# Attention scores from one matmul of full 32-bit operands, in place of three of high and low parts

## The chip, the cores and the metric

The kernel runs on one core of one Trainium2 chip. The metric is the device time of one execution in microseconds (us). The core has five engines that run side by side and meet only at semaphores: TensorE (PE in the rows; its weight loads are PEld), VectorE (DVE), ScalarE (ACT), GpSimd (POOL) and SyncE (SP), which here only issues DMAs.

## The reference

`x` is 64 sequences of 512 rows by 512 features; the context is 64 x 77 rows by 512. What is computed, cut to the parts that matter:

```
h      = layernorm(x)
q      = h @ Wq          16 query heads of 32, in 4 groups for each of 4 key heads
k, v   = ctx @ Wk, ctx @ Wv      4 heads of 32
scores = rope(q) . rope(k)       queries summed over their group; 77 context rows for each head
o      = mean over heads of softmax(scores / sqrt(32)) @ v
x1     = x + o @ Wo
x2     = x1 + ffn(layernorm(x1))     8-bit inputs, weights of -1, 0, 1, one global scale
```

## The kernel before, in words

The work has three stages, one after the other, as the program on each engine is written by hand.

**The context stage** runs over 39 tiles of 128 context rows (the last has 64). For each tile TensorE transposes the context (L1054), multiplies it by the weights of keys and values (L1065, 12 matmuls, also of high and low parts, which the change does not touch), and transposes the rotated keys (L1073). ScalarE copies the transposed keys out of PSUM as float32r, a form that is rounded to fewer mantissa bits and takes one matmul record (`keys_out`, L595): this is the high part. VectorE subtracts it from the full value in PSUM and keeps the rest as the low part (`low_keys`, L787). SyncE stores both to the scratch tensor `k_scr` (L331 in the loop, L365 at its end), after it has stored the values (L330), and loads the context four tiles ahead (L324). SyncE does all of this in the order of the program.

**The attention stage** runs over 128 steps, each a pair of 128-row tiles of `x`. It is a software pipeline: in step i, projection works on pair i, scores on i-1, values on i-2, the head sum on i-3, the residual on i-4, and statistics on i-5. TensorE's order within a step is: transposes of `x` (L1138), of rotated queries (L1150) and of the attention output (L1158), the query projection (L1168, full 32-bit), the output projection (L1179), transposes of the exponentials (L1189), the scores (L1203), the value products (L1216, full 32-bit). The scores of a pair are two PSUM banks, one for each tile, 308 columns wide: 4 heads x 77 context rows, with the keys laid out block-diagonally in `k_blk`. Each bank takes three matmuls: high query x low key, low x high, high x high. The high query part is ScalarE's copy (L653), the low part VectorE's subtraction (L912), which also signals `qlo_ready`. SyncE loads the keys of each sequence into `k_blk` in four pieces (L400), one for each head, and the values in six (L404).

**The last stage** quantises, transposes, and multiplies by the ternary weights (f16, L1248). It reads nothing that the change touches.

`low_keys` is called once for each context tile, and L912 once for each step of the attention stage.

Of the kernel before, what the change touches and what calls it, by code (L numbers as in the profile page):

```python
# [32 lines left out]
CTX = 77  # L33
HEADS, GROUPS, D = 4, 4, 32
HD = HEADS * D

P = 128
# [6 lines left out]
SC = HEADS * CTX  # L44
# [46 lines left out]
def build(nc, x, ctx_in, wq, wk, wv, wo, fw, fb, ident_d, qcos_d, qsin_d, kcos_d, ksin_d, out):  # L91
# [11 lines left out]
    with stack:  # L103
        def sb(name, shape, dt=F32):
            return stack.enter_context(nc.sbuf_tensor(name, shape, dt))
# [4 lines left out]
        def sem(name):  # L110
            return stack.enter_context(nc.semaphore(name))


        k_scr = nc.dram_tensor("k_scr", (P, 2, CROWS), F32, kind="Internal").ap()
        v_scr = nc.dram_tensor("v_scr", (CROWS, HEADS, VC), F32, kind="Internal").ap()


# [8 lines left out]
        q_sb = sb("q_sb", [P, 2 * HD])  # L126
        qa_sb = sb("qa_sb", [P, 2 * HD])
        qb_sb = sb("qb_sb", [P, 2 * HD])
        qT_sb = sb("qT_sb", [P, 2, 2 * P], F32R)
        e_sb = sb("e_sb", [P, 2, 2, SC])  # L130
        pT_sb = sb("pT_sb", [P, 2, CHUNKS * P])
        pv_sb = sb("pv_sb", [P, 2, HEADS, VC])
# [3 lines left out]
        ost_sb = sb("ost_sb", [P, 2, 2, 2, D], F32R)  # L136
        oT_sb = sb("oT_sb", [P, 2, P], F32R)
        sq_sb = sb("sq_sb", [P, E], BF16)
        k_blk = sb("k_blk", [P, 2, 2, SC])
        v_blk = sb("v_blk", [P, 2, CHUNKS, HEADS, VC])  # L140
        bn_sb = sb("bn_sb", [P, 2, 6])
        mv_sb = sb("mv_sb", [P, 2, 2])
# [48 lines left out]
        ka_sb = early(2, HD)  # L191
        kb_sb = early(2, HD)
        kr_sb = early(2, HD)
        kT_sb = early(2, 2, P)
        kT_r = kT_sb.bitcast(F32R)
        v_sb = early(4, HEADS, VC)
        vw_sb = early(2, HEADS, D)
        wo4 = early(E)
# [38 lines left out]
        cT_done, cT_copied, kv_done, kr_ready, v_ready, v_copied, kT_done, kT_copied, kv_read = (  # L237
            sem(n) for n in ("cT_done", "cT_copied", "kv_done", "kr_ready", "v_ready", "v_copied",
                             "kT_done", "kT_copied", "kv_read"))
        k_copied, k_mul, klo_ready, qlo_ready = (sem(n) for n in ("k_copied", "k_mul", "klo_ready", "qlo_ready"))  # L240
        whi_ready, wlo_ready, clo_ready = sem("whi_ready"), sem("wlo_ready"), sem("clo_ready")

        stats_ready, rs_ready = sem("stats_ready"), sem("rs_ready")
# [64 lines left out]
        def _(sp):  # L308
# [15 lines left out]
                sp.dma_start(ctx_sb[0:rows, n, :], ctx_rows[bass.ds((j + 4) * P, rows), :]).then_inc(c_in[n], 16)  # L324

            def kv_store(j, n):
                sp.wait_ge(klo_ready, j - 1)
                sp.wait_ge(v_copied, j + 1)
                sp.wait_ge(v_ready, j + 1)
                sp.dma_start(v_scr[bass.ds(j * P, P), :, :], v_sb[:, n, :, :]).then_inc(v_out[n], 16)  # L330
                sp.dma_start(k_scr[:, :, bass.ds((j - 2) * P, P)], kT_sb[:, n % 2, :, :])\  # L331
                  .then_inc(k_out[n % 2], 16)

            sp.wait_ge(zeroed, ZEROED)
# [22 lines left out]
            for j in range(groups * 4, CT + 3):  # L357
                if j + 4 <= CT:
                    ctx_load(j, j % 4, P if j + 4 < CT else CLAST)
                if j in (CT - 5, CT - 2):  # L360
                    b = 1 + (j == CT - 2)
                    sp.dma_start(x_sb[:, b, :, :], xv[b]).then_inc(x_in[b], 16)
                rows = P if j - 2 < CT else CLAST
                sp.wait_ge(klo_ready, j - 1)
                sp.dma_start(k_scr[:, :, (j - 2) * P:(j - 2) * P + rows], kT_sb[:, j % 2, :, 0:rows])\  # L365
                  .then_inc(k_out[j % 2], 16)
                if j <= CT:
                    rows = P if j < CT else CLAST
                    sp.wait_ge(v_copied, j + 1)
                    sp.wait_ge(v_ready, j + 1)  # L370
                    sp.dma_start(v_scr[j * P:j * P + rows, :, :], v_sb[0:rows, j % 4, :, :])\
                      .then_inc(v_out[j % 4], 16)
# [23 lines left out]
            def kv_step(b, k):  # L396

                at_least(sp, sc_done_t, 4 * (b - 2) + 4)
                for h in range(HEADS):
                    sp.dma_start(k_blk[D * h:D * h + D, k % 2, :, CTX * h:CTX * h + CTX],  # L400
                                 k_scr[D * h:D * h + D, :, bass.ds(b * CTX, CTX)]).then_inc(k_in[k % 2], 16)
                at_least(sp, pv_done, 2 * (b - 2) + 2)
                for c, r, n, h, a in SEGS:
                    sp.dma_start(v_blk[r:r + n, k % 2, c, h, :], v_scr[bass.ds(b * CTX + a, n), h, :])\  # L404
                      .then_inc(v_in[k % 2], 16)
# [52 lines left out]
        def _(pool):  # L458
            pool.memset(ones_sb[:, :], 1.0).then_inc(zeroed, 1)
            pool.memset(v_sb[:, :, :, D + 1:D + 2], 1.0).then_inc(zeroed, 1)  # L460
            pool.memset(k_blk[:, :, :, :], 0.0).then_inc(zeroed, 1)
            pool.memset(v_blk[:, :, :, :, :], 0.0).then_inc(zeroed, 1)
            pool.memset(mhalf[:, :], -0.5).then_inc(zeroed, 1)
            pool.memset(bones[:, :], 0.0).then_inc(zeroed, 1)
# [97 lines left out]
        def _(act):  # L562
# [26 lines left out]
            def keys_out(j, m, g, rows=P):  # L589

                act.wait_ge(kT_done, j + 1)

                at_least(act, k_out[m], 16 * g)

                act.activation(kT_r[:, m, 0, 0:rows], bank[4 + m][:, 0:rows], ACT.Copy).then_inc(kT_copied, 1)  # L595

            ctx_step(0, 0)
            for j in range(4):
# [24 lines left out]
            def step(i, k, g):  # L623
# [21 lines left out]
                if score:  # L645
                    j, kj, gj = score
                    act.wait_ge(qT_done, j + 1)
                    if resid:

                        act.wait_ge(oT_done, resid[0] + 1)  # L650

                    at_least(act, sc_done_t, 2 * j)
                    act.activation(qT_sb[:, 0, :], bank[3][:, 0:2 * P], ACT.Copy).then_inc(qT_copied, 1)  # L653
                if resid:
                    j, kj, gj = resid
                    act.wait_ge(oT_done, j + 1)
# [79 lines left out]
        def _(dve):  # L736
# [44 lines left out]
                dve.tensor_reduce(v_sb[0:rows, n, :, D:D + 1].rearrange("p h a -> p (h a)"),  # L781
                                  vw_sb[0:rows, n % 2, :, :], AX.X, ALU.add).then_inc(v_ready, 1)

            def low_keys(j, n, rows=P):

                dve.wait_ge(kT_copied, j + 1)
                dve.tensor_tensor(kT_r[:, n, 1, 0:rows], bank[4 + n][:, 0:rows], kT_sb[:, n, 0, 0:rows],  # L787
                                  ALU.subtract).then_inc(klo_ready, 1)

            wq_groups = [wq_sb[:, :, :, g, :].rearrange("p c h d -> p (c h) d") for g in range(GROUPS)]  # L790
            wq_sum = wqs[:, :, :].rearrange("p c (h d) -> p (c h) d", h=HEADS)
            for j in range(CHEAD):
                if j >= 1:
                    low_ctx(j + 1, (j + 1) % 2)
                ctx_step(j, j % 4, j // 4)
                if j >= 2:
                    low_keys(j - 2, j % 2)

                if j == 5:
                    dve.wait_ge(wq_in, 16)  # L800
                    then(dve.tensor_tensor(wq_sum, wq_groups[0], wq_groups[1], ALU.add))
# [31 lines left out]
            with dve.Fori(CHEAD // 4, CTAIL // 4) as g:  # L833
                for n in range(4):
                    low_ctx(g * 4 + n + 1, (n + 1) % 2)
                    ctx_step(g * 4 + n, n, g)
                    low_keys(g * 4 + n - 2, n % 2)
            for j in range(CTAIL, CT + 3):
                if j < CT:
                    low_ctx(j + 1, (j + 1) % 2, P if j + 1 < CT else CLAST)  # L840
                if j <= CT:
                    ctx_step(j, j % 4, j // 4, P if j < CT else CLAST)
                if j - 2 < CT:
                    low_keys(j - 2, j % 2)
                o = j - CTAIL
                if o == 0:

# [18 lines left out]
            def step(i, k, g):  # L866
# [20 lines left out]
                if proj:  # L887
                    j, kj, gj = proj
                    dve.bn_stats(bn_sb[:, 1, :], x_sb[:, kj // 2, 2 * (kj % 2) + 1, :]).then_inc(bn_step, 1)  # L889
                    if isinstance(j, int) and j == 0:  # L890

                        low_keys(CT, CT % 2, CLAST)
                    dve.wait_ge(bn_step, 2 * j + 2)
                if stat:

# [9 lines left out]
                if score:  # L905

                    j, kj, gj = score
                    if resid:
                        dve.wait_ge(oT_copied, resid[0] + 1)
                    else:  # L910
                        dve.wait_ge(qT_copied, j + 1)
                    dve.tensor_tensor(qT_sb[:, 1, :], bank[3][:, 0:2 * P], qT_sb[:, 0, :].bitcast(F32),  # L912
                                      ALU.subtract).then_inc(qlo_ready, 1)
                if proj:
                    j, kj, gj = proj

# [128 lines left out]
        def _(pe):  # L1045
# [23 lines left out]
            def ctx_kT(j, n, rows=P):  # L1069
                m = n % 2  # L1070
                pe.wait_ge(kr_ready, j + 1)
                at_least(pe, klo_ready, j - 1)
                pe.transpose(bank[4 + m][:, 0:rows], kr_sb[0:rows, m, :], ident[0:rows, 0:rows])\  # L1073
                  .then_inc(kT_done, 1)

# [49 lines left out]
            def step(i, k, g):  # L1125
# [66 lines left out]
                if score:  # L1192
                    j, kj, gj = score
                    slot = kj // 2 % 2
                    if kj % 2 == 0:

                        pe.wait_ge(k_in[slot], gj * (2 * K_DMAS * 16) + (kj // 4 + 1) * (K_DMAS * 16))

                    at_least(pe, sub_done_t, 2 * j)
                    pe.wait_ge(qlo_ready, j + 1)  # L1200
                    for t in range(2):
                        for n, (a, b) in enumerate(((0, 1), (1, 0), (0, 0))):
                            last = pe.matmul(bank[4 + t][:, 0:SC], qT_sb[:, a, t * P:(t + 1) * P],  # L1203
                                             k_blk[:, slot, b, :].bitcast(F32R), start=n == 0, stop=n == 2)
                        last.then_inc(sc_done_t, 1)
                if value:
                    j, kj, gj = value
                    slot = kj // 2 % 2
# [100 lines left out]
```

## Time and profile before

| | |
|---|---|
| median of 3 runs | 1320.23 us (1318.98 to 1321.29) |
| the profiled execution's own time | 1319.5 us |
| its span, first to last instruction | 1317.7 us |
| mean granted TensorE clock | 0.99 of full speed |
| PE busy | 1267.9 us (96%), x9848 |
| PEld busy | 1085.9 us (82%), x9911 |
| DVE busy | 1181.8 us (90%), x2772 |
| ACT busy | 1025.1 us (78%) |
| POOL busy | 791.2 us (60%) |

The spans of records on one engine overlap in the trace, since matmuls and vector operations are pipelined. So the distance from start to start tells what a record costs its engine, and the record's own duration does not. A full 32-bit matmul of the program stands as two records in the trace: the query projection is 128 x 2 x 4 = 1024 matmuls of the program and x2048 records.

### The profile page before, as it was taken

Reading aid. Unit: us, or ns where it says so; the run is one execution under the profiler, and the core shown is the slowest. Engines: PE = TensorE matmul, PEld = TensorE weight load, DVE = VectorE, ACT = ScalarE, POOL = GpSimd, SP = SyncE. Lnnn points to the kernel's source line nnn. Section 1 sums busy time; section 2 is a strip of 40 time slices with the busy share of each in tenths; the row PEclk is TensorE's granted clock in tenths of the full one; section 3 lists DMA queues with packets and bytes.
Section 4 is the critical chain, followed back from the end, with each engine's and each line's share of the span. In section 5 each row is a group of like instructions: output and inputs, shape, how many; then the busy total and the mean of one; then the engine's idle time right before and its main releaser. Section 6 shows DMA issues by size and latency. Waiting matters only on the chain.

```text
span 1317.7 us, 36811 instructions
## 1 busy us (share of the span) xinstructions
PE 1267.9 (96%) x9848; PEld 1085.9 (82%) x9911; DVE 1181.8 (90%) x2772; ACT 1025.1 (78%) x2338; POOL 791.2 (60%) x1536
## 2 busy tenths in 40 slices
PE   5897999999999999999999999999969999999998
PEld 5796999999999999999999999999935555555554
DVE  4876899999999999999999999999978888888887
ACT  3454788888888888888888888888857878888886
POOL 3564888888888888888888888888820000000000
PEclk9999999999999999999999999999979999999999
DMA  8574355555555555555546452323108999999945
GB/s 266 166 216 133 107 158 182 154 183 161 176 165 171 165 171 167 170 171 166 178 159 187 150 169 76 102 80 98 37 5 332 400 401 395 401 399 404 406 201 223
DMA packets 100815, 265.18 MB, mean 201 GB/s; under 512 B 49705, under 2 KB 65769, under 8 KB 72114
## 3 DMA queue, kind: packets, MB, share of 16 engines
q1 hardware_dynamic: 100786, 264.86, 58.8%
q8 instruction: 10, 0.16, 0.1%
q14 instruction: 19, 0.16, 0.0%
HBM read 139.64 MB, written 125.17 MB: 201 GB/s over the span
## 4 chain that ended last, share of the span: by engine, by line
DVE 47%; PE 31%; issue 15%; DMA 2%; DVEq 2%; SPq 1%; ACT 1%; POOL 1%; POOLq 0%; ACTq 0%
PE bank L1248 18%; DVE amax L898 10%; DVE x_sb L930 8%; DVE e_sb L944 6%; DVE mx_sb L940 5%; DVE bn_sb L889 5%; PE bank L1239 4%; PE bank L1246 3%; DVE qT_sb L912 2%; PE bank L1065 2%; DVE rinv_sb L886 2%; DVE ve_sb L918 2%; DVE bn_sb L881 2%; DVE mv_sb L904 1%; DMA x_sb<-in_ctx 1%
## 5 line engine op out<-in xcount | busy, mean ns | idle before, releaser
L1248 PE MATMUL bank<-wT,x_sb 128*128 128x512 f16 x1024 | 263.9, 380 | 3.5 <-issue 0.2
L1168 PE MATMUL bank<-wqs,xT_sb 128*128 128x128 f32 x2048 | 259.7, 280 | 0.2
L718 ACT ACTIVATE x_sb<-bank,mean,cols 128x512 f32<-128x512 f32 x256 | 196.0, 774 | 67.6 <-PE bank L1248 67.3
L1168 PEld LDWEIGHTS bank<-wqs,xT_sb 128*128 128x128 f32 x2048 | 238.2, 191 | 7.1 <-ACT xT_sb L640 0.8
L1216 PE MATMUL bank<-v_blk,pT_sb 103*128 103x136 f32 x1536 | 199.0, 279 | 0.3 <-ACT pT_sb L682 0.3
L1216 PEld LDWEIGHTS bank<-v_blk,pT_sb 103*128 103x128 f32 x1536 | 190.6, 190 | 0.5 <-ACT pT_sb L682 0.5
L1248 PEld LDWEIGHTS bank<-wT,x_sb 128*128 128x128 f16 x1024 | 100.5, 98 | 106.8 <-issue 1.6
L930 DVE SCALAR_TENSOR_TENSOR x_sb<-x_sb,negm,bank 128x512 f32 (+1 forms) x256 | 179.5, 742 | 7.9 <-PE bank L1179 2.7
L898 DVE TENSOR_REDUCE amax<-x_sb (+1 forms) x128 | 156.0, 1218 | 23.2 <-DVE bn_sb L889 8.0
L691 ACT ACTIVATE sq_sb<-x_sb 128x512 bf16 (+1 forms) x256 | 161.4, 631 | 18.7 <-DVE x_sb L930 1.4
L1005 DVE TENSOR_TENSOR x_sb<-x_sb 128x512 f32 (+1 forms) x256 | 164.5, 683 | 1.2 <-ACT x_sb L718 1.2
L682 ACT ACTIVATE pT_sb<-bank 103x384 f32<-103x384 f32 x256 | 111.7, 489 | 53.1 <-PE bank L1189 53.1
L640 ACT ACTIVATE xT_sb<-bank 128x512 f32<-128x512 f32 x256 | 138.9, 595 | 7.6 <-PE bank L1138 3.0
L1203 PE MATMUL bank<-k_blk,qT_sb 128*128 128x308 f32 x768 | 140.1, 317 | 1.8 <-DMA k_blk<-k_scr 1.8
L504 POOL TENSOR_TENSOR rs<-ve_sb,mhalf 128x2 f32 (+1 forms) x128 | 89.5, 700 | 79.9 <-DVE ve_sb L875 79.9
L1138 PE MATMUL bank<-ident,x_sb 128*128 128x128 f32 x1024 | 133.0, 273 | 0.0
L667 ACT ACTIVATE e_sb<-e_sb,rs_sb 128x308 f32<-128x308 f32 x256 | 129.2, 568 | 0.0
L997 DVE TENSOR_SCALAR x_sb<-bank 128x1024 f16<-128x1024 f16 x128 | 88.5, 691 | 44.6 <-PE bank L1239 43.0
L940 DVE TENSOR_REDUCE mx_sb<-bank 128x4 f32<-128x308 f32 x256 | 110.1, 471 | 11.0 <-PE bank L1203 8.1
L1138 PEld LDWEIGHTS bank<-ident,x_sb 128*128 128x128 f32 x1024 | 117.0, 141 | 0.0
L1203 PEld LDWEIGHTS bank<-k_blk,qT_sb 128*128 128x128 f32 x768 | 111.0, 189 | 2.2 <-DMA k_blk<-k_scr 2.0
L1189 PEld LDWEIGHTS bank<-ident,e_sb 128*103 128x103 f32 x768 | 98.5, 168 | 15.4 <-issue 1.3
(126 smaller groups left out, 2584.4 us busy)
## 6 DMA issues: line engine op xcount, KB each, us to landing
out_y<-x_sb SPq DMA_DIRECT2D x112, 1024.0 KB, 7.2
x_sb<-in_x SPq DMA_DIRECT2D x64, 1024.0 KB, 6.5
x_sb<-out_y SPq DMA_DIRECT2D x48, 1024.0 KB, 9.0
x_sb<-in_ctx SPq DMA_DIRECT2D x38, 256.0 KB, 2.8
k_blk<-k_scr SPq DMA_DIRECT2D x256, 19.2 KB, 5.5
k_scr<-x_sb SPq DMA_DIRECT2D x38, 128.0 KB, 2.3
v_scr<-x_sb SPq DMA_DIRECT2D x38, 68.0 KB, 2.3
v_blk<-v_scr SPq DMA_DIRECT2D x128, 10.2 KB
```

Source lines behind the costliest of these rows:

```text
L640: act.activation(xT_sb[:, t, :, :].rearrange("p c r -> p (c r)"), bank[t][:, :], ACT.Copy).then_inc(xT_copied_t, 1)
L691: act.activation(sq_sb[:, :], x1_at(kj, gj, t), ACT.Square, accum_out=ssq[:, bass.ds(2 * j + t, 1)]).then_inc(sq_done, 1)
L718: act.activation(u_sb[:, t, :], bank[4 + t][:, :], ACT.Identity, bias=stat_of(mean1, j, t, back), scale=cols[:, 6:7]).then_inc(scaled_t, 1)
L898: dve.tensor_reduce(amax[:, bass.ds(2 * j, 2)], x1_at(kj, gj).rearrange("p (t e) -> p t e", t=2), AX.X, ALU.max, apply_absolute_value=True ...
L930: dve.scalar_tensor_tensor(out=x1_at(kj, gj, t), in0=x_sb[:, kj // 2, 2 * (kj % 2) + t, :], scalar=negm[:, kj, t:t + 1], in1=bank[t][:, :] ...
L940: dve.tensor_reduce(mx_sb[:, t, :], bank[4 + t][:, 0:SC].rearrange("p (h a) -> p h a", h=HEADS), AX.X, ALU.max).then_inc(mx_ready, 1)
L1005: dve.tensor_tensor(x1_tile, x1_tile, u_sb[:, t, :], ALU.add).then_inc(sum_done_t, 1)
L1138: last = pe.transpose(bank[t][:, c * P:(c + 1) * P], x_sb[:, kj // 2, 2 * (kj % 2) + t, c * P:(c + 1) * P], ident[:, :])
L1168: last = pe.matmul(bank[2][:, t * HD:(t + 1) * HD], xT_sb[:, t, c, :], wqs[:, c, :], start=c == 0, stop=c == EC - 1)
L1203: last = pe.matmul(bank[4 + t][:, 0:SC], qT_sb[:, a, t * P:(t + 1) * P], k_blk[:, slot, b, :].bitcast(F32R), start=n == 0, stop=n == 2)
L1216: last = pe.matmul(bank[6][:, t * HEADS * VC:(t + 1) * HEADS * VC], pT_sb[0:CR, t, c * P:(c + 1) * P], v_blk[0:CR, slot, c, :, :].rearrang ...
L1248: last = pe.matmul(bank[4 + t][:, :], q16T_sb[:, t, c, :], wT[:, c, :], start=False, stop=c == EC - 1)
```

## The change

The keys and queries are no longer split. `kT_sb`, `k_scr`, `k_blk` and `qT_sb` lose the dimension that held the two parts, and hold plain float32. `low_keys` and the subtraction of L912 are gone from VectorE, with their semaphores `klo_ready` and `qlo_ready`; whoever waited for these now waits for ScalarE's copies, `kT_copied` and `qT_copied`. The scores of each tile are one matmul of float32 operands.

```diff
-        k_scr = nc.dram_tensor("k_scr", (P, 2, CROWS), F32, kind="Internal").ap()
+        k_scr = nc.dram_tensor("k_scr", (P, CROWS), F32, kind="Internal").ap()
...
-        qT_sb = sb("qT_sb", [P, 2, 2 * P], F32R)
+        qT_sb = sb("qT_sb", [P, 2 * P])
...
-        k_blk = sb("k_blk", [P, 2, 2, SC])
+        k_blk = sb("k_blk", [P, 2, SC])
...
             def kv_store(j, n):
-                sp.wait_ge(klo_ready, j - 1)
+                sp.wait_ge(kT_copied, j - 1)
...
-                sp.dma_start(k_scr[:, :, bass.ds((j - 2) * P, P)], kT_sb[:, n % 2, :, :])\
+                sp.dma_start(k_scr[:, bass.ds((j - 2) * P, P)], kT_sb[:, n % 2, :])\
...
-                    sp.dma_start(k_blk[D * h:D * h + D, k % 2, :, CTX * h:CTX * h + CTX],
-                                 k_scr[D * h:D * h + D, :, bass.ds(b * CTX, CTX)]).then_inc(k_in[k % 2], 16)
+                    sp.dma_start(k_blk[D * h:D * h + D, k % 2, CTX * h:CTX * h + CTX],
+                                 k_scr[D * h:D * h + D, bass.ds(b * CTX, CTX)]).then_inc(k_in[k % 2], 16)
...
-                act.activation(kT_r[:, m, 0, 0:rows], bank[4 + m][:, 0:rows], ACT.Copy).then_inc(kT_copied, 1)
+                act.activation(kT_sb[:, m, 0:rows], bank[4 + m][:, 0:rows], ACT.Copy).then_inc(kT_copied, 1)
...
-                    act.activation(qT_sb[:, 0, :], bank[3][:, 0:2 * P], ACT.Copy).then_inc(qT_copied, 1)
+                    act.activation(qT_sb[:, :], bank[3][:, 0:2 * P], ACT.Copy).then_inc(qT_copied, 1)
...
-            def low_keys(j, n, rows=P):
-
-                dve.wait_ge(kT_copied, j + 1)
-                dve.tensor_tensor(kT_r[:, n, 1, 0:rows], bank[4 + n][:, 0:rows], kT_sb[:, n, 0, 0:rows],
-                                  ALU.subtract).then_inc(klo_ready, 1)
...
-                    if resid:
-                        dve.wait_ge(oT_copied, resid[0] + 1)
-                    else:
-                        dve.wait_ge(qT_copied, j + 1)
-                    dve.tensor_tensor(qT_sb[:, 1, :], bank[3][:, 0:2 * P], qT_sb[:, 0, :].bitcast(F32),
-                                      ALU.subtract).then_inc(qlo_ready, 1)
...
-                at_least(pe, klo_ready, j - 1)
+                at_least(pe, kT_copied, j - 1)
...
-                    pe.wait_ge(qlo_ready, j + 1)
-                    for t in range(2):
-                        for n, (a, b) in enumerate(((0, 1), (1, 0), (0, 0))):
-                            last = pe.matmul(bank[4 + t][:, 0:SC], qT_sb[:, a, t * P:(t + 1) * P],
-                                             k_blk[:, slot, b, :].bitcast(F32R), start=n == 0, stop=n == 2)
-                        last.then_inc(sc_done_t, 1)
+                    pe.wait_ge(qT_copied, j + 1)
+                    for t in range(2):
+                        pe.matmul(bank[4 + t][:, 0:SC], qT_sb[:, t * P:(t + 1) * P], k_blk[:, slot, :],
+                                  start=True, stop=True).then_inc(sc_done_t, 1)
```

TensorE, in a full step of the attention stage, from the output projection to the first value product; before:

```order
L1179 MATMUL bank<-wst,oT_sb 128x512 [waits oT_copied]
L1179 MATMUL bank<-wst,oT_sb 128x512
L1189 MATMUL bank<-ident,e_sb 103x128 [waits exp_done_t,pv_copied]
L1189 MATMUL bank<-ident,e_sb 103x128 x5
L1203 MATMUL bank<-k_blk,qT_sb 128x308 [waits qlo_ready,sub_done_t]
L1203 MATMUL bank<-k_blk,qT_sb 128x308 x5
L1216 MATMUL bank<-v_blk,pT_sb 128x136 [waits pT_copied_t,v_in1]
```

The same place in the changed kernel, whose line numbers are smaller:

```order
L1154 MATMUL bank<-wst,oT_sb 128x512 [waits oT_copied]
L1154 MATMUL bank<-wst,oT_sb 128x512
L1164 MATMUL bank<-ident,e_sb 103x128 [waits exp_done_t,pv_copied]
L1164 MATMUL bank<-ident,e_sb 103x128 x5
L1177 MATMUL bank<-k_blk,qT_sb 128x308 [waits qT_copied,sub_done_t]
L1177 MATMUL bank<-k_blk,qT_sb 128x308
L1189 MATMUL bank<-v_blk,pT_sb 128x136 [waits pT_copied_t,v_in1]
```

Six matmuls of the program have become two at the same place, and nothing else in the step has moved.

VectorE, in the same steady step, from the maximum of absolute values (L898) to the row maximum of the scores (L940); before:

```order
L898 TENSOR_REDUCE amax<-x_sb 128x2 [waits added_t,bn_step]
L904 BN_AGGR mv_sb<-bn_sb 128x2 x2
L912 TENSOR_TENSOR qT_sb<-bank,qT_sb 128x256 [waits oT_copied]
L918 TENSOR_SCALAR ve_sb<-mv_sb 128x2 [waits mv_ready]
L920 TENSOR_SCALAR negm<-mv_sb 128x2
L930 SCALAR_TENSOR_TENSOR x_sb<-x_sb,negm,bank 128x512 [waits y_done_t]
```

In the changed kernel, at that place:

```order
L882 TENSOR_REDUCE amax<-x_sb 128x2
L888 BN_AGGR mv_sb<-bn_sb 128x2 x2
L893 TENSOR_SCALAR ve_sb<-mv_sb 128x2 [waits mv_ready]
L895 TENSOR_SCALAR negm<-mv_sb 128x2
```

The subtraction and its wait are gone, and the two small operations behind it have moved up.

SyncE, in the loop of the context stage: a context load, the store of the values, and the store of the keys; before:

```order
L324 DMA x_sb<-in_ctx 128x512
L330 ISA [waits v_ready,v_copied,klo_ready]
L330 DMA v_scr<-x_sb 128x136
L331 ISA
L331 DMA k_scr<-x_sb 256x1x128
```

In the changed kernel:

```order
L323 DMA x_sb<-in_ctx 128x512
L329 ISA [waits v_ready,v_copied,kT_copied]
L329 DMA v_scr<-x_sb 128x136
L330 ISA
L330 DMA k_scr<-x_sb 128x128
```

The store of the keys has half as many rows, and the wait ahead of the store of the values asks for ScalarE's copy in place of VectorE's subtraction.

## Rows read from the trace of the kernel before

**Rows 1.** Windows: us, busy us (records) of each engine, granted clock, DMA share, GB/s
```profile
0.00:126.00 126.00, 98.81 (x750) 91.46 (x751) 83.92 (x209) 55.49 (x169) 63.08 (x136) 0.97 0.68 203
126.00:955.00 829.00, 827.80 (x6817) 805.86 (x6815) 791.55 (x2014) 690.24 (x1757) 720.14 (x1384) 1.00 0.48 147
...
977.00:1317.00 340.00, 331.26 (x2233) 181.98 (x2294) 290.46 (x510) 267.81 (x382) 0.00 (x0) 0.99 0.86 346
```

**Rows 2.** Waits from 300 to 900 us: total us, times, longest us
```profile
ACT pv_sb L631 <- PE bank L1216: 22.0, 92, 0.3
ACT q_sb L674 <- PE bank L1168: 20.5, 91, 0.2
```

**Rows 3.** The chain from 147.5 to 156 us: start us, us, what
```profile
147.80 0.47 PE bank L1179 x2
148.27 0.65 PE bank L1189 x6
148.92 0.86 PE bank L1203 x6
149.78 1.39 PE bank L1216 x12
151.17 0.88 PE bank L1138 x8
152.05 0.22 PE bank L1150 x2
...
152.49 1.86 PE bank L1168 x16
```

**Rows 4.** The page's chain by engine, over the whole span
```profile
DVE 47%; PE 31%; issue 15%; DMA 2%; DVEq 2%; SPq 1%; ACT 1%; POOL 1%; POOLq 0%; ACTq 0%
```

**Rows 5.** VectorE's timeline in one step: start us, us, line, operation
```profile
600.11 0.39 DVE L912 TENSOR_TENSOR qT_sb<-bank,qT_sb 128x256 fp32r<-128x256 f32 x1
600.42 0.30 DVE L918 TENSOR_SCALAR ve_sb<-mv_sb 128x2 f32<-128x2 f32 x1
...
600.84 1.41 DVE L930 SCALAR_TENSOR_TENSOR x_sb<-x_sb,negm,bank 128x512 f32 x2
602.24 0.86 DVE L940 TENSOR_REDUCE mx_sb<-bank 128x4 f32<-128x308 f32 x2
...
606.64 0.39 DVE L912 TENSOR_TENSOR qT_sb<-bank,qT_sb 128x256 fp32r<-128x256 f32 x1
```

**Rows 6.** TensorE's timeline in the same step
```profile
601.03 1.10 PE L1203 MATMUL bank<-k_blk,qT_sb 128*128 128x308 f32 x6
```

**Rows 7.** Groups by line and shape: records | busy us, mean ns | idle before
```profile
L1248 PE MATMUL bank<-wT,x_sb 128*128 128x512 f16 x1024 | 263.9, 380 | 3.5 <-issue 0.2
...
L1216 PE MATMUL bank<-v_blk,pT_sb 103*128 103x136 f32 x1536 | 199.0, 279 | 0.3 <-ACT pT_sb L682 0.3
L1203 PE MATMUL bank<-k_blk,qT_sb 128*128 128x308 f32 x768 | 140.1, 317 | 1.8 <-DMA k_blk<-k_scr 1.8
...
L1239 PE MATMUL bank<-ident,x_sb 128*128 128x128 f16 x1024 | 78.9, 220 | 2.5 <-ACT x_sb L708 2.3 <-DVE x_sb L1015 0.2
```

**Rows 8.** The chain from 0 to 126 us, shares by line
```profile
by line: PE bank L1065 18.6%; DMA x_sb<-in_ctx 12.7%; DVE cT_parts L753 6.4%; PE bank L1054 6.4%; issue 5.4%; DVE x_sb L776 4.7%; DMA x_sb<-in_wv 3.9%; DVE x_sb L787 3.3%; DMA k_scr<-x_sb 3.3%; DVE x_sb L781 3.1%; SPq L331 2.7%; DVE x_sb L8
```

**Rows 9.** SyncE's timeline in the context stage
```profile
86.41 0.35 SPq L330 DMA_DIRECT2D v_scr<-x_sb  x1
86.94 0.59 SPq L331 DMA_DIRECT2D k_scr<-x_sb  x1
```

**Rows 10.** SyncE's timeline at the start of the attention stage
```profile
120.45 2.61 SPq L400 DMA_DIRECT2D k_blk<-k_scr  x4
123.10 2.29 SPq L404 DMA_DIRECT2D v_blk<-v_scr  x6
```

More of the change, by code:

```diff
@@ L193, in build @@
         kr_sb = early(2, HD)
-        kT_sb = early(2, 2, P)
-        kT_r = kT_sb.bitcast(F32R)
+        kT_sb = early(2, P)
         v_sb = early(4, HEADS, VC)
@@ L239, in build @@
                              "kT_done", "kT_copied", "kv_read"))
-        k_copied, k_mul, klo_ready, qlo_ready = (sem(n) for n in ("k_copied", "k_mul", "klo_ready", "qlo_ready"))
+        k_copied, k_mul = sem("k_copied"), sem("k_mul")
         whi_ready, wlo_ready, clo_ready = sem("whi_ready"), sem("wlo_ready"), sem("clo_ready")
@@ L363, in _ @@
                 rows = P if j - 2 < CT else CLAST
-                sp.wait_ge(klo_ready, j - 1)
-                sp.dma_start(k_scr[:, :, (j - 2) * P:(j - 2) * P + rows], kT_sb[:, j % 2, :, 0:rows])\
+                sp.wait_ge(kT_copied, j - 1)
+                sp.dma_start(k_scr[:, (j - 2) * P:(j - 2) * P + rows], kT_sb[:, j % 2, 0:rows])\
                   .then_inc(k_out[j % 2], 16)
@@ L460, in _ @@
             pool.memset(v_sb[:, :, :, D + 1:D + 2], 1.0).then_inc(zeroed, 1)
-            pool.memset(k_blk[:, :, :, :], 0.0).then_inc(zeroed, 1)
+            pool.memset(k_blk[:, :, :], 0.0).then_inc(zeroed, 1)
             pool.memset(v_blk[:, :, :, :, :], 0.0).then_inc(zeroed, 1)
@@ L795, in _ @@
                 ctx_step(j, j % 4, j // 4)
-                if j >= 2:
-                    low_keys(j - 2, j % 2)
                 if j == 5:
@@ L836, in _ @@
                     ctx_step(g * 4 + n, n, g)
-                    low_keys(g * 4 + n - 2, n % 2)
             for j in range(CTAIL, CT + 3):
@@ L842, in _ @@
                     ctx_step(j, j % 4, j // 4, P if j < CT else CLAST)
-                if j - 2 < CT:
-                    low_keys(j - 2, j % 2)
                 o = j - CTAIL
@@ L889, in step @@
                     dve.bn_stats(bn_sb[:, 1, :], x_sb[:, kj // 2, 2 * (kj % 2) + 1, :]).then_inc(bn_step, 1)
-                    if isinstance(j, int) and j == 0:
-                        low_keys(CT, CT % 2, CLAST)
                     dve.wait_ge(bn_step, 2 * j + 2)
@@ L904, in step @@
                         dve.bn_aggr(mv_sb[:, t, :], bn_sb[:, t, :]).then_inc(mv_ready, 1)
-                if score:
-                    j, kj, gj = score
-                    if resid:
-                        dve.wait_ge(oT_copied, resid[0] + 1)
-                    else:
-                        dve.wait_ge(qT_copied, j + 1)
-                    dve.tensor_tensor(qT_sb[:, 1, :], bank[3][:, 0:2 * P], qT_sb[:, 0, :].bitcast(F32),
-                                      ALU.subtract).then_inc(qlo_ready, 1)
                 if proj:
```

## The prediction

> **What bounds the kernel now.** I read the windows first, to know which stage the change falls in. The attention stage fills 829 of the 1317.7 us, and in it TensorE is busy for 827.80 at a granted clock of 1.00, which is the level of 2.4 GHz [rows 1]. The last stage, 340 us, touches nothing that is changed. Next the waits: over 600 us of the attention stage ScalarE waits for TensorE at two places in nearly every step, 0.2 us at each [rows 2], and no row has TensorE waiting for anyone. Then the chain, where it runs through TensorE: the pieces of a step follow each other without a gap, and L1203 is one of them with 0.86 us [rows 3] (0.85 in other steps). The pieces add up to one step: 0.47 + 0.65 + 0.86 + 1.39 + 0.88 + 0.22 + 0.22 (L1158, the same as L1150) + 1.86 = 6.55 us.
>
> Against this stands the chain over the whole span, which gives VectorE 47% and TensorE 31% [rows 4]. VectorE is busy for 791.55 of the 829 us [rows 1], so the two engines run neck and neck. Which one holds the other is to be seen in one step: the scores' records end at 601.03 + 1.10 = 602.13, and VectorE's row maximum, which needs them, starts at 602.24 [rows 5, 6]. The operation before it, L930, ends at 600.84 + 1.41 = 602.25. VectorE is thus released by TensorE at about the moment at which it would be free anyway, and its next wait is so short that it shows as no gap. I take TensorE as the engine that sets the step: its pieces stand at the pace of their columns and it waits for nobody.
>
> **The scores, the term that decides.** Now they are six records of 308 columns: 0.855 us for six, 0.1425 each [rows 3]. After, each program matmul of full 32-bit operands is two records, so there are four in a step. No row has such a record of 308 columns. The nearest is the value product, L1216, with 136 columns: 1.39 / 12 = 0.116 us from start to start [rows 3]. Is that pace set by the columns, and how often do they pass? The durations tell: f16 records take 220 ns with 128 columns and 380 with 512, so 0.417 ns for each column [rows 7]. A single pass of 136 columns would be 220 + 8 x 0.417 = 223 ns; the row has 279, which is 220 + 144 x 0.417 = 280, that is 272 columns. So a record of full 32-bit operands passes its columns twice. The pace agrees: 272 x 0.417 = 113 ns and some 2.5 ns more is the 116 seen. For 308 columns this gives 616 x 0.417 + 2.5 = 259 ns; scaled in proportion from L1216 it would be 0.116 x 308 / 136 = 0.262. I take 0.260: four records take 1.04 us in place of 0.855, so 0.185 us more a step, and 128 x 0.185 = **+23.7 us**.
>
> Two pages of the Trainium skill speak to this and don't agree. "FP8 and Floating Point Precision", section "TensorE Precision Notes", has true FP32 pass the array four times, which would make the sum what it is. "Perfetto Trace Analysis", section "Engine Utilization", only halves the output rate for FP32_LOW_HIGH; read as two passes for the whole matmul, it would make this change a gain (rival 1).
>
> **Bounds of that term.** Below: 616 x 0.417 with nothing on top, 257 ns, gives 4 x 0.257 - 0.86 = 0.168 a step, +21.5 us. Above: the one-pass records that the kernel has now are slower than their columns, 0.1425 where 308 x 0.417 + 2.5 is 0.131, so by 9%. L1216 shows no such loss, but it is short. With 9% on 259 the record is 0.282, and the step 0.273 longer: +35 us.
>
> **The wait before the scores.** TensorE waited for `qlo_ready`, now for `qT_copied`, which comes sooner. The subtraction ends at 600.11 + 0.39 = 600.50 and the scores start at 601.03 [rows 5, 6], so nothing hung on it. No gain.
>
> **VectorE.** It loses L912, which holds it for 0.31 us a step (L912 starts at 600.11, the next operation at 600.42) [rows 5]. Its own work fits in a step already, and TensorE's step grows to 6.55 + 0.185 = 6.73. So this becomes idle time: L930 may start earlier only if the output projection is done, and the row maximum must wait for the scores, which come 0.185 later. Late next after the maximum are the reciprocal for GpSimd and the statistics; both move with TensorE's step. Gain 0. If VectorE were the true bound, see rival 3.
>
> **The context stage.** Here TensorE is busy for 98.81 of 126 us [rows 1], and other work on the chain shrinks. The subtraction L787 holds 3.3% of 126 us, 4.2 us, and it goes wholly. The issue of the store of keys, L331, holds 2.7%, 3.4 us [rows 8]. It takes 0.59 us where the value store, which has 128 rows as the new one will, takes 0.35 [rows 9]: 0.24 / 0.59 of 3.4 is 1.4 us. At the start of the attention stage four loads of keys take 2.61 us to issue, 0.65 each, and those of values 2.29 / 6 = 0.38 [rows 10]; three of them stand on the chain ahead of the first scores: 3 x 0.27 = 0.8 us. Together 6.4 us if all of it is kept. Not all will be: where L787 goes, L1065 or a context load is late next. Nothing kept would be the other bound. I keep 4.5 us, about two thirds, since TensorE has slack of about a fifth there: **-4.5 us**. Loads and stores of keys move half the bytes; in the attention stage DMA is busy for 0.48 of the time [rows 1] and nobody on TensorE waits for it, so that is 0.
>
> **The sum.** 1319.5 us (the profiled execution) + 23.7 - 4.5 = 1338.7. The median of the runs is 0.7 us above the profiled one, so 1339.4; I say 1339.5 us, +1.5%.
>
> **Rivals.**
> 1. *Full 32-bit records pass their columns once, and their pace so far is set by the weight load.* For it: all records of 128 and 136 columns stand at 0.110 to 0.116 us (0.88 / 8, 1.39 / 12), as if by a common floor [rows 3]. Against it: the durations of 279 against 220 ns [rows 7]. Then a record of 308 columns costs what it does now, 0.1425, and four 0.57: -0.285 a step, -36.5 us, and 1320.2 - 36.5 - 4.5 = 1279 us. It decides from a pace below 0.855 / 4 = 0.214 us for the stage alone, and 0.214 + 4.5 / 512 = 0.223 with the context stage's gain. This is what the halved rate of "Perfetto Trace Analysis" would bring; the durations of this trace speak against it. Chance 5%.
> 2. *The long record loses 9% as the one-pass records do.* 1320.2 + 35 - 3 = 1352 us. Against it: L1216 at its columns' pace. Chance 9%.
> 3. *VectorE holds the step today.* For it: its 47% of the chain [rows 4] and 791.55 of 829 us. Then its 0.31 us fall out, and TensorE's own floor decides. In a step that is 6.55 less the one slack that its pieces show: L1168's 1.86 against 16 records of 256 x 0.417 + 2.5 = 109 ns, so 0.115. Then 6.435 + 0.185 = 6.62, +0.07 a step, +9 us: 1320.2 + 9 - 4.5 = 1325 us. Chance 8%.
> 4. *No difference:* a pace near 0.22 us, for which no row speaks. 2%.
>
> **Chances and range.** My forecast has 76%, with a range of its own of 1334 to 1343 us (term of the scores 21.5 to 26, the context stage 2 to 6.4). Reaching part of the way to rivals 3 and 2, since between them and the forecast mixtures can lie, the range is 1329 to 1347 us; what it leaves out is rival 1, most of 2 and 3, and 4, under 2 in 10 with what the mixtures hold back. A measurement of this kernel can tell about 0.2%, 2.6 us, from no change. Faster by more than that: 5% (rival 1). Within it: 3% (rival 4, and a little for a sum of small errors). Slower: 92%.
>
> **What would show each step.** In the changed kernel's trace: the scores as x512 records in all, 259 to 262 ns from start to start, with a mean duration near 430 (220 + 488 x 0.417 = 423 and a little for the first of a step); in the chain, four records with 1.04 us; a step of 6.73 us; TensorE without waits, and VectorE with a new wait of 0.1 to 0.3 us a step at the row maximum or at L930, for TensorE; the stage of the context shorter by 2 to 6 us, with the store of keys issued in about 0.36 us. I am wrong if the four records take 0.6 us (rival 1) or 1.13 (rival 2), or if the step is shorter than 6.55 + 0.15 although the records are as foretold (rival 3).

## The result, and the profile after

| | before | changed |
|---|---|---|
| median | 1319.61 us (1318.84 to 1321.29, 4 runs) | 1336.53 us (1334.67 to 1339.28, 4 runs) |
| profiled execution | 1319.5 us | 1337.84 us |
| span | 1317.7 us | 1336.0 us |
| VectorE busy | 1181.8 us | 1161.8 us |

The ratio is 1.0127, with a 95% interval of 1.0114 to 1.014: 15 to 18.5 us slower. The forecast was 1339.5 us, in a range of 1329 to 1347.

The chain of the changed kernel, one step of the attention stage (start us, us, what):

```profile
606.67 0.88 PE bank L1113 x8
607.55 0.22 PE bank L1125 x2
607.76 0.22 PE bank L1133 x2
607.98 1.87 PE bank L1143 x16
609.85 0.47 PE bank L1154 x2
610.31 0.66 PE bank L1164 x6
610.97 1.04 PE bank L1177 x4
612.01 1.39 PE bank L1189 x12
613.40 0.11 PE bank L1113
```

Against [rows 3] one piece has changed: the scores are four records with 1.04 us, where six had 0.86. From one group of transposes of `x` to the next it is 613.40 - 606.67 = 6.73 us, against 6.55.

The page of the changed kernel, its chain over the whole span, and the groups of the scores and of VectorE's row maximum:

```profile
PE 92%; DVE 3%; DMA 1%; issue 1%; ACT 1%; POOL 1%; SPq 1%; POOLq 0%; DVEq 0%; ACTq 0%
...
L1177 PE MATMUL bank<-k_blk,qT_sb 128*128 128x308 f32 x512 | 153.9, 423 | 0.0
...
L915 DVE TENSOR_REDUCE mx_sb<-bank 128x4 f32<-128x308 f32 x256 | 110.6, 474 | 36.9 <-PE bank L1177 34.4
```

The same place of the kernel before, from its view of L940 (what VectorE sat idle for ahead of the row maximum: us, times):

```profile
  PE bank L1203: 8.1, 6
```

The chain has moved from VectorE (47% in [rows 4]) to TensorE. VectorE now waits for the scores, 34.4 us in all. In the kernel before it had 8.1 us of this wait, at 6 places; in the other steps the wait was too short to be told from the end of L930. One step of VectorE in the changed kernel shows the new wait:

```profile
603.73 1.40 DVE L905 SCALAR_TENSOR_TENSOR x_sb<-x_sb,negm,bank 128x512 f32 x2
605.39 0.86 DVE L915 TENSOR_REDUCE mx_sb<-bank 128x4 f32<-128x308 f32 x2 [0.25 <-PE bank L1177]
```

To part the stages, take the first and the last group of transposes of `x` in the attention stage. TensorE's timeline before:

```profile
113.76 1.04 PE L1138 MATMUL bank<-ident,x_sb 128*128 128x128 f32 x8
...
943.98 1.04 PE L1138 MATMUL bank<-ident,x_sb 128*128 128x128 f32 x8
```

and in the changed kernel:

```profile
110.79 1.04 PE L1113 MATMUL bank<-ident,x_sb 128*128 128x128 f32 x8
...
963.07 1.04 PE L1113 MATMUL bank<-ident,x_sb 128*128 128x128 f32 x8
```

The attention stage starts 3.0 us earlier. Its 127 steps take 852.28 us in place of 830.22: 22.1 us more, 0.174 a step. What lies behind the last group is 372.9 us in place of 373.7. So -3.0 + 22.1 - 0.8 = +18.3 us, the difference of the spans.

The first steps fill the pipeline and differ from the rest. In the middle, from 300 to 900 us, the mean step is 6.551 us before and 6.728 in the changed kernel: 0.177 more. The scores and the transposes ahead of them can be parted from the other pieces. In one step, TensorE's timeline before and then changed:

```profile
148.11 0.82 PE L1189 MATMUL bank<-ident,e_sb 128*103 128x128 f32 x6
...
149.62 1.55 PE L1216 MATMUL bank<-v_blk,pT_sb 103*128 103x136 f32 x12
```

```profile
145.99 0.82 PE L1164 MATMUL bank<-ident,e_sb 128*103 128x128 f32 x6
...
147.68 1.55 PE L1189 MATMUL bank<-v_blk,pT_sb 103*128 103x136 f32 x12
```

From the first of these starts to the second is 1.51 and 1.69 us. Over the 90 steps in the middle the means are 1.508 and 1.693 us, so the scores cost 0.185 us more. The output projection ahead of them, from its start to that of the transposes, takes 0.555 and 0.547 us, which gives 0.008 back.

SyncE in the changed kernel, in the context stage and at the start of the attention stage:

```profile
80.27 0.34 SPq L329 DMA_DIRECT2D v_scr<-x_sb  x1
80.80 0.34 SPq L330 DMA_DIRECT2D k_scr<-x_sb  x1
...
115.00 1.74 SPq L399 DMA_DIRECT2D k_blk<-k_scr  x4
```

The store of keys is issued in 0.34 us in place of 0.59 [rows 9], four loads of keys in 1.74 in place of 2.61 [rows 10].

### The profile page after: what moved, and what is told of

It is laid out like the page before. It is cut to its first block, busy times and chain, and to the rows that moved or that the text cites. A ratio compares the mean times of both kernels' runs of the same rounds, so it can differ in the third digit from the quotient of the medians.

```text
span 1336.0 us, 36113 instructions
## 1 busy us (share of the span) xinstructions
PE 1289.9 (97%) x9592; PEld 1075.9 (81%) x9655; DVE 1161.8 (87%) x2605; ACT 1025.0 (77%) x2338; POOL 790.1 (59%) x1536
## 4 chain that ended last, share of the span: by engine, by line
PE 92%; DVE 3%; DMA 1%; issue 1%; ACT 1%; POOL 1%; SPq 1%; POOLq 0%; DVEq 0%; ACTq 0%
PE bank L1143 18%; PE bank L1221 17%; PE bank L1189 13%; PE bank L1177 10%; PE bank L1113 8%; PE bank L1164 6%; PE bank L1154 4%; PE bank L1212 4%; PE bank L1219 3%; PE bank L1040 2%; PE bank L1125 2%; PE bank L1133 2%; DMA x_sb<-in_ctx 1%; PE bank L1029 1%; DVE cT_parts L752 1%
## 5 line engine op out<-in xcount | busy, mean ns | idle before, releaser
L1189 PEld LDWEIGHTS bank<-v_blk,pT_sb 103*128 103x128 f32 x1536 | 197.1, 190 | 18.0 <-ACT pT_sb L681 0.5
L1189 PE MATMUL bank<-v_blk,pT_sb 103*128 103x136 f32 x1536 | 199.2, 279 | 0.3 <-ACT pT_sb L681 0.3
L1177 PE MATMUL bank<-k_blk,qT_sb 128*128 128x308 f32 x512 | 153.9, 423 | 0.0
L915 DVE TENSOR_REDUCE mx_sb<-bank 128x4 f32<-128x308 f32 x256 | 110.6, 474 | 36.9 <-PE bank L1177 34.4
L919 DVE TENSOR_TENSOR e_sb<-bank,mx_sb 128x308 f32<-128x308 f32 x256 | 109.4, 470 | 0.0
```

Source lines behind the costliest of these rows:

```text
L1177: pe.matmul(bank[4 + t][:, 0:SC], qT_sb[:, t * P:(t + 1) * P], k_blk[:, slot, :], start=True, stop=True).then_inc(sc_done_t, 1)
L1189: last = pe.matmul(bank[6][:, t * HEADS * VC:(t + 1) * HEADS * VC], pT_sb[0:CR, t, c * P:(c + 1) * P], v_blk[0:CR, slot, c, :, :].rearrang ...
```

## The experiments

Theory T: TensorE sets the step, and the time follows from the pace of its score records; what VectorE is freed from stays hidden. The first rival, V, is that VectorE held the step before. Each ratio is against the kernel before, timed beside the experiment (medians 1320.2 to 1320.4 us).

### VectorE's subtraction put back

```diff
+                if score:
+                    j, kj, gj = score
...
+                    dve.tensor_tensor(qlo_sb[:, :], bank[3][:, 0:2 * P], qT_sb[:, :],
+                                      ALU.subtract).then_inc(qlo_ready, 1)
...
-                    pe.wait_ge(qT_copied, j + 1)
+                    pe.wait_ge(qlo_ready, j + 1)
```

> The changed kernel with VectorE's subtraction of the queries put back: it reads the same bank, writes a tile that nobody reads, and TensorE waits for it ahead of the scores as before. The scores stay one full 32-bit matmul for each tile. Theory T (TensorE sets the step, VectorE's 0.31 us a step were and are hidden): the step stays at 6.73 us and the time at that of the changed kernel, 1336.5 us within 2. Rival V (VectorE sets or shares the step, so that freeing it gave something back): the step grows by 0.1 to 0.3 us, the time by 13 to 38 us to 1350 or more.

1335.66 us, ratio 1.0122 (1.0107 to 1.0138); the changed kernel has 1.0127. The operation costs nothing where it stood. Rival V falls on this side.

### The subtraction taken from the kernel before

```diff
-                    dve.tensor_tensor(qT_sb[:, 1, :], bank[3][:, 0:2 * P], qT_sb[:, 0, :].bitcast(F32),
-                                      ALU.subtract).then_inc(qlo_ready, 1)
...
-                    pe.wait_ge(qlo_ready, j + 1)
+                    pe.wait_ge(qT_copied, j + 1)
...
-                        for n, (a, b) in enumerate(((0, 1), (1, 0), (0, 0))):
+                        for n, (a, b) in enumerate(((0, 1), (0, 0), (0, 0))):
```

> The kernel before with the subtraction of the queries taken out and nothing else moved: still six one-pass records in a step, of which the second of each tile takes the high query part and the high keys in place of the low part and the high keys, so the low part of the queries is left out and the main product counts twice. Theory T: VectorE only hugged TensorE, so the step stays at 6.55 us and the time at 1319.6 within 2; the chain over the span moves from VectorE to TensorE. Rival V: VectorE held the step, its 0.31 us fall out and TensorE's floor of 6.44 decides, so 1305 us.

1318.68 us, ratio 0.9993 (0.9982 to 1.0004): no difference. Its page, the chain over the span:

```profile
PE 87%; DVE 6%; DMA 2%; issue 2%; SPq 1%; ACT 1%; POOL 1%; DVEq 0%; POOLq 0%; ACTq 0%
```

With the time unchanged, the chain went from 47% VectorE to 87% TensorE. So the 47% of [rows 4] said that VectorE had no visible gap, not that it held the step.

### The attention stage changed alone

```diff
-                        for n, (a, b) in enumerate(((0, 1), (1, 0), (0, 0))):
-                            last = pe.matmul(bank[4 + t][:, 0:SC], qT_sb[:, a, t * P:(t + 1) * P],
-                                             k_blk[:, slot, b, :].bitcast(F32R), start=n == 0, stop=n == 2)
-                        last.then_inc(sc_done_t, 1)
+                        pe.matmul(bank[4 + t][:, 0:SC], qT_sb[:, t * P:(t + 1) * P], k_blk[:, slot, 0, :],
+                                  start=True, stop=True).then_inc(sc_done_t, 1)
```

> The kernel before with the attention stage alone changed: full 32-bit queries, one full 32-bit matmul for each tile, no subtraction of the queries. The context stage stays as before: keys split, both parts stored and loaded; the low part of the keys is loaded and not used. Theory T: the attention stage as in the changed kernel, step 6.73 us, and the context stage as in the kernel before, its first transposes of x 3.0 us later than in the changed kernel (113.8 us against 110.8 in the two traces), so 1339.5 us. Rival C (those 3 us are chance of one profile and the two stages differ by nothing): the same as the changed kernel, 1336.5. Rival D (halved key loads helped the attention stage): a step longer than 6.73.

1341.39 us, ratio 1.0177 (1.0161 to 1.0193), 5.7 us over the first experiment, which was timed beside it and differs from it by the keys and by the hidden subtraction. That is more than the 3.0 us expected. Its attention stage starts at 113.31 us, that one's at 110.22. Over all profiles with unsplit keys (nine) the start lies at 110.2 in the mean, over those with split keys (five) at 113.8: the context stage is 3.6 us shorter. The start varies from profile to profile, from 107.3 to 111.5 us with unsplit keys and from 113.3 to 114.5 with split ones, but the two groups don't overlap. The steady step is 6.733 us against 6.726, under a microsecond in all, so rival D has at most that there. The first four steps take 24.8 us against 23.2, which is 1.6 us more. This is not shown to come from the loads of keys: the changed kernel, whose loads are halved as well, takes 24.8 us for them too. The medians lie 1 us further apart than the two profiled spans, which is within the spread of the runs.

### Each score matmul in two halves, and in four quarters

```diff
-                        pe.matmul(bank[4 + t][:, 0:SC], qT_sb[:, t * P:(t + 1) * P], k_blk[:, slot, :],
-                                  start=True, stop=True).then_inc(sc_done_t, 1)
+                        for c in range(2):
+                            last = pe.matmul(bank[4 + t][:, c * (SC // 2):(c + 1) * (SC // 2)],
+                                             qT_sb[:, t * P:(t + 1) * P],
+                                             k_blk[:, slot, c * (SC // 2):(c + 1) * (SC // 2)],
+                                             start=True, stop=True)
+                        last.then_inc(sc_done_t, 1)
```

and with 4 in place of 2.

> The changed kernel with each full 32-bit score matmul cut into two of 154 columns: eight records in a step in place of four, with the same columns in all and twice the weight loads. Theory T (pace is 2 x columns x 0.417 ns and about 2.5 ns): a record is 131 ns, eight are 1.05 us against 1.04, the step grows by 0.01 us, the time by 1 to 2 us. Rival L (a record costs by its weight load or a fixed price, with columns counted once): eight records cost up to twice four, so up to 1 us more a step and 100 us more.

> The changed kernel with each full 32-bit score matmul cut into four of 77 columns: sixteen records in a step. By columns alone a record would be 2 x 77 x 0.417 + 2.5 = 67 ns and sixteen 1.07 us. But all records with 128 weight columns of 32 bits in the trace stand at 109 ns or more, also transposes whose columns would allow it if they passed once. Theory T with a floor for the weight load of 0.109: sixteen take 1.74 us, the step grows by 0.70 us to 7.43, the time by 90 us to 1427. Rival F (no floor, columns alone): the step grows by 0.03, the time by 4 us.

Halves: 1337.53 us (ratio 1.0137, 1.0122 to 1.0153), 131 ns a record. Quarters: 1430.7 us (1.0839, 1.0823 to 1.0856). The pieces of the scores in the chain and their records (duration in ns: min/median/max), of the halves and then of the quarters:

```profile
604.95 1.05 PE bank L1178 x8
...
L1178 PE MATMUL bank<-k_blk,qT_sb x1024: 292/294/398, 121.5 to 975.4; 128*128 128x154 f32 x171
```

```profile
609.20 1.74 PE bank L1178 x16
...
L1178 PE MATMUL bank<-k_blk,qT_sb x2048: 232/275/398, 117.5 to 1065.7; 128*128 128x77 f32 x187
```

1.05 / 8 = 0.131 us for 154 columns is 308 x 0.417 + 2.5 ns: the columns count twice, and the number of records and weight loads nothing. 1.74 / 16 = 0.109 for 77 columns is not 154 x 0.417 + 2.5 = 67 ns but a floor. So both regimes exist, and records of 308 columns are far from the floor.

That the floor is the weight load is not shown. "TensorE: Matmul & The Clock Gate" of the Trainium skill, section "LDWEIGHTS (loading the stationary operand)", prices a load by its columns, which is 107 ns for 128; the pace of 109 lies near that. But the load's own record in this run lasts 192 ns, every load here has 128 columns, and no run changed that number, so a fixed price of a 32-bit record would look the same. The transposes, at 0.88 / 8 = 0.110 in [rows 3], decide nothing: their own 128 columns, passed twice, give 256 x 0.417 + 2.5 = 109 ns as well.

### Two products, with and without the subtraction

```diff
-                        for n, (a, b) in enumerate(((0, 1), (1, 0), (0, 0))):
+                        for n, (a, b) in enumerate(((0, 1), (0, 0))):
```

The second of the two runs also has the subtraction taken out, as above.

> The kernel before with two one-pass products in place of three: high queries by low keys and high by high; the product of the low query part with the high keys is left out, while VectorE still makes the low part. TensorE loses 2 x 0.1425 = 0.285 us a step. Theory T would give 6.55 - 0.285 = 6.27 us a step if nothing else is near; VectorE's own operations fill about 6.4 to 6.5 of a step with the subtraction in it, so I expect it to take over at 6.4 to 6.5 and the time to fall by 7 to 20 us to 1300 to 1312. If VectorE had room, 1283.

> As the run before, with the subtraction of the queries on VectorE taken out as well (left out: the low part of the queries). Theory T: TensorE 6.27 us a step, VectorE's operations without the subtraction some 6.15 to 6.25, so the step is 6.27 to 6.3 and the time 1283 to 1288. If VectorE's subtraction is what held the run before, the difference between the two runs shows it, up to 0.2 us a step.

1294.49 us (ratio 0.9799, 0.9785 to 0.9812) and 1286.14 us (0.9741, 0.9728 to 0.9754). The first is below the 1300 to 1312 us that I had expected. Most steps are 6.28 and 6.27 us: TensorE's 6.55 - 0.285, with the subtraction too. So VectorE, which I had put at 6.4 to 6.5 us, had about 0.27 us or more to spare in most steps of the kernel before. The mean steps are 6.35 and 6.28. The difference sits where the loop turns, once in eight steps: with the subtraction two steps there take some 6.70 and 6.42 us, 13.1 together, which is what two steps of the kernel before take, so there VectorE had hardly any room left. Without the subtraction one step of some 6.36 us is all that remains. In the first of the two runs TensorE waits for the subtraction there, and its weight load ahead of the scores stands idle; the waits from 155 to 950 us:

```profile
PEld bank L1203 <- issue: 5.6, 15, 0.4
PE bank L1203 <- DVE qT_sb L912: 2.8, 14, 0.3
```

### One product

```diff
-        qT_sb = sb("qT_sb", [P, 2 * P])
+        qT_sb = sb("qT_sb", [P, 2 * P], F32R)
...
-                        pe.matmul(bank[4 + t][:, 0:SC], qT_sb[:, t * P:(t + 1) * P], k_blk[:, slot, :],
-                                  start=True, stop=True).then_inc(sc_done_t, 1)
+                        pe.matmul(bank[4 + t][:, 0:SC], qT_sb[:, t * P:(t + 1) * P], k_blk[:, slot, :].bitcast(F32R),
+                                  start=True, stop=True).then_inc(sc_done_t, 1)
```

> The changed kernel with keys and queries rounded to one-pass form: one one-pass matmul for each tile, two records in a step (left out: both low parts). TensorE: 6.73 - 1.04 + 0.285 = 5.97 us a step. If TensorE still set the step, 1336.5 - 97 = 1240 us. But VectorE's own operations need some 6.15 to 6.25 us, so I expect it to be the bound: a step of 6.2 and 1268 to 1275 us.

1276.35 us, ratio 0.9672 (0.9656 to 0.9688): faster than both kernels. Most steps take 6.21 us; the mean is 6.25, since a few take 6.28 and one in eight some 6.44. The size is close to what I expected, but I had given VectorE as the reason, and the next run was made to test that:

```diff
-                    dve.wait_ge(bn_step, 2 * j + 2)
...
+                    dve.wait_ge(bn_step, 2 * j + 2)
+                    dve.tensor_scalar(spare[:, :], cols[:, 1:2], 1.0, None, ALU.mult)
```

The wait moves from ahead of the maximum of absolute values to behind it. The same edit was made on the changed kernel.

> The run with one one-pass product, with one more edit: VectorE's wait for its own two statistics operations stands behind the maximum of absolute values in place of ahead of it, on a one-column operation that is added there. The low parts of keys and queries are left out as in that run. In that run's trace VectorE has no wait for TensorE and idles 0.18 us a step at the maximum, for itself. Theory W (VectorE's own sequence is what sets the step of 6.215 us there): 0.18 less some 0.07 for the added operation, so 6.10 us a step and 1262 us in place of 1276. Rival P (GpSimd or TensorE's waits for ScalarE set it): no change beyond 3 us.

> The changed kernel with the same edit alone. Theory T (TensorE sets the step): VectorE's 0.1 us are hidden, 1336.5 us within 2, with a longer wait of VectorE for TensorE. If VectorE had a share in the step, up to 14 us less.

1275.73 us (ratio 0.9665, 0.9652 to 0.9678) and 1336.6 us (1.0122, 1.0106 to 1.0137): neither moved. Theory W falls. VectorE got its time and only waits longer: in the first of the two, 0.2 us a step at L907, for the output projection. The chain of the run with one product and the wait in its old place shows what its step is made of:

```profile
604.39 0.46 PE bank L1154 x2
604.85 0.66 PE bank L1164 x6
605.51 0.28 PE bank L1177 x2
605.79 1.63 PE bank L1189 x12
```

The value product is 1.63 us and no longer 1.39. Its weights are ScalarE's copy of the transposed exponentials. The scores stand between these transposes and the value product; with 1.04 or 0.86 us they cover the copy (0.49 us for the first half, started when the first three transposes are done), with 0.28 they don't. In this step the first copy starts at 605.22 and so ends at 605.71, and the first weight load of the value product starts at 605.76. 6.727 - 1.04 + 0.285 + 0.24 = 6.21. That weight load, and the waits of that run from 300 to 900 us:

```profile
605.76 0.53 PEld L1189 LDWEIGHTS bank<-v_blk,pT_sb 103*128 103x128 f32 x4 [0.22 <-ACT pT_sb L681]
...
PEld bank L1189 <- ACT pT_sb L681: 13.2, 60, 0.2
PEld bank L1189 <- issue: 10.2, 36, 0.3
```

### The output projection between the transposes and the value product

```diff
-                if resid:
-
-                    j, kj, gj = resid
-                    pe.wait_ge(oT_copied, j + 1)
...
                 if value:
...
+                if resid:
+
+                    j, kj, gj = resid
+                    pe.wait_ge(oT_copied, j + 1)
```

The whole block of L1179 moves behind the transposes of L1189.

> The run with one one-pass product and the later wait on VectorE, with one more edit: TensorE's output projection (0.47 us) stands behind the transposes of the exponentials in place of ahead of them. The low parts of keys and queries are left out as in that run. There, the piece of the value product in the chain was 1.63 us in place of 1.39: TensorE waited 0.24 us a step for ScalarE's copy of the transposed exponentials, which the longer scores had covered. Theory K (this wait is all that keeps the step at 6.21 and not at 5.97): the projection covers it, the step is 5.97 to 6.0 and the time 1243 to 1250 us. Rival (VectorE, released later by the projection and with 6.0 us of its own work, is late next): 6.05 to 6.15, so 1255 to 1268.

> The same edit on the run with one one-pass product, with VectorE's wait where it was (left out: both low parts). If Theory K holds and VectorE's own sequence of some 6.0 to 6.2 us is late next, this one is slower than its twin by up to 0.1 us a step, 13 us; if VectorE has room, both are 1243 to 1250 us.

1322.24 us (ratio 1.0012, 1.0004 to 1.0021) and 1322.5 us (1.0008, 0.9999 to 1.0017): both 46 us slower than without the move, and outside all that was expected. The wait for the copy went (the value product takes 1.39 us again), and a worse one came. The waits of the first of these runs, 300 to 900 us:

```profile
DVE x_sb L907 <- PE bank L1167: 45.8, 45, 1.1
PEld bank L1127 <- POOL qa_sb L554: 44.8, 46, 1.0
```

and pieces of its chain:

```profile
600.04 0.74 DVE x_sb L907
600.78 0.78 DVE mx_sb L917 x2
...
602.25 0.17 DVE ve_sb L863
...
602.57 0.61 POOL rs L504
603.24 0.64 POOL pw_sb L510
603.95 0.42 POOL pw_sb L515
604.37 0.66 POOL rs_sb L521
...
607.80 0.74 POOL qa_sb L554
...
608.58 0.44 PE bank L1127 x2
...
611.88 0.48 PE bank L1167 x2
...
613.30 0.74 DVE x_sb L907
```

The projection comes 0.65 us later, so VectorE's addition (L907), its row maximum and its small operation L863 do too. On that operation GpSimd's whole sequence of some 6 us waits, whose last product, the rotated queries, TensorE transposes next. Behind them come the query projection and the output projection, for which VectorE's addition waits again. This closes a ring over all three engines. From L907 at 600.04 to L907 at 613.30 one round takes 13.26 us, and it spans two steps: in the middle of the run one step takes some 6.15 us and the next some 7.05, 6.60 in the mean. This ring was not among my rivals.

Theory K is thus not shown. Without the wait for the copy even the shorter steps take some 6.15 us and not 5.97; what else stands in them no run was made for.

## Why the prediction was right, point by point

- **TensorE sets the step.** Right, and shown from both sides: the subtraction back costs nothing, the subtraction away gives nothing. The reading that decided was VectorE's start at the row maximum beside the end of the scores [rows 5, 6], against the larger number of [rows 4].
- **The scores' term, +0.185 us a step, +23.7 us.** The mechanism is right, and so is the size: a record of 308 columns is 0.259 us from start to start and 423 ns long, which are the numbers of the working, and the scores cost 0.185 us more a step (1.693 against 1.508). The step grew a little less, by 0.177 in the middle, since the output projection ahead of the transposes took 0.008 less, a term that the prediction doesn't have; why is open. Over all 127 steps, the first ones with them, it is 0.174 a step and 22.1 us.
- **Full 32-bit operands pass their columns twice in each record.** Shown by the halves: 154 columns take 0.131 us, 308 take 0.259. The prediction had read it from the 279 ns of the value product's records, against 223 for a single pass. That reading was less safe than it looked: by the same formula the records of the quarters, 77 columns passed twice, would last 220 + 26 x 0.417 = 231 ns, and their median is 275. At the floor of 0.109 us a record is thus longer than its columns make it, so the 279 ns at 136 columns did not exclude rival 1. The conclusion came out right, with some luck. So a full 32-bit matmul costs four passes against three of one each, and the one-pass records give back part of it, since they run 9% slower than their columns: 4 x 308 x 0.417 = 514 ns for each tile against 3 x 142 = 427. "FP8 and Floating Point Precision" of the Trainium skill, section "TensorE Precision Notes", is right with its four passes; the halved rate of "Perfetto Trace Analysis", section "Engine Utilization", fits one record of two passes and not the whole matmul.
- **Rival 1, a price by weight load,** did not come at 308 columns. A floor of 0.109 us exists, shown by the quarters; whether the weight load sets it is open.
- **Rival 2, 9% on the long record,** did not come: 0.259.
- **Rival 3, VectorE,** fell; its room was 0.27 us or more in most steps.
- **The wait ahead of the scores, no gain.** Right by the first experiment, which put the later wait back.
- **VectorE's new wait, 0.1 to 0.3 us.** 0.25 at the row maximum in the step shown.
- **The context stage, -4.5 us.** The size was a little off: 3.0 us in the two profiles, 3.6 over fourteen. The issue times came as computed (0.34, and 0.44 for each load of keys, not quite the 0.38 taken from the values' loads). Of the 6.4 us that were worked out from the chain about half was kept. What took the rest was not tested.
- **The sum.** For the profiled execution it was 1338.7, and 1337.84 was measured. It lies closer than its terms do: the attention stage gave 1.6 us less than forecast and the context stage kept 1.5 us less, which cancel, and 0.8 us fell away behind the last group of transposes, for which there was no term. Between the medians the miss is 3 us: the prediction added 0.7 us from the profiled execution to the median, and the changed kernel's profiled execution was 1.3 us above its median.

VectorE's 0.31 us a step brought nothing, because VectorE was not the engine that was waited for.

## What to carry to other kernels

Before three one-pass products are merged into one full 32-bit matmul, count columns and not instructions: three passes against four. As long as a record's columns take longer than its floor (0.109 us here), fewer records bring nothing. An engine that holds a large share of the chain without gaps may only hug the one that sets the pace; look at one step, at what it waits for and when it would have been free, or take an operation away from it. And a piece of work in an in-order queue is also the cover of the wait behind it: with the scores shortened so far that they no longer covered ScalarE's copy, TensorE waited 0.24 us a step, and the obvious filler made another ring longer.

The fastest version measured is the one with one one-pass product, 1276 us; it leaves out the low parts of keys and queries. With the low part of the keys kept it is 1286 us.

## What the runs showed of the hardware that was not expected

One-pass records of 32-bit operands run slower than f16 ones of equal width: 142 ns for 308 columns where 131 would be the f16 pace, 0.47 / 2 = 0.235 us for 512 [rows 3] against 0.215 for the f16 records of 512 in the last stage, which the chain of the kernel before has in pieces of four of 0.86 us. The two-pass records show no such loss, at 136, 154 or 308 columns. The cause stays open; no run here was made for it.
